# Row-maximum products in four row groups, a scalar form of the mask product, and a new order of the second pass in a four-layer graph network

## The reference

```python
h = jnp.maximum(_layernorm(x, axis=-1), 0.0)
Q = (h @ Wq.T).reshape(b, n, H, DH).transpose(0, 2, 1, 3)      # H = 8, DH = 32; K and V likewise
scores = jnp.einsum('bhnd,bhmd->bhnm', Q, K) / jnp.sqrt(jnp.float32(DH))
scores = jnp.where(adj[:, None, :, :] == 0, -jnp.inf, scores)
attn = jax.nn.softmax(scores, axis=-1)
out = jnp.einsum('bhnm,bhmd->bhnd', attn, V)
x = x + out.transpose(0, 2, 1, 3).reshape(b, n, H * DH) @ Wo.T + bo
```

## Time and profile before

| what | value |
|---|---|
| median of 3 runs | 3994.09 us (3990.95 to 3995.72) |
| span of the profiled execution | 3982.8 us |
| PE busy | 3709.5 us, 93% |
| DVE busy | 3101.9 us, 78% |
| ACT busy | 1994.8 us, 50% |
| POOL busy | 1576.2 us, 40% |
| share of PE in the chain that ended last | 78% |

### The profile page before, as it was taken

One profiled execution on the slowest core, in us unless ns is written; L12 is line 12 of the kernel. 1 busy time (PEld: TensorE's weight loads), 2 busy tenths in 40 slices (PEclk: granted clock), 3 DMA queues, 4 the chain that ended last, 5 costly groups with the idle time before them and its releaser, 6 DMA issues.

```text
span 3982.8 us, 59433 instructions
## 1 busy us (share of the span) xinstructions
PE 3709.5 (93%) x19042; PEld 2707.6 (68%) x19042; DVE 3101.9 (78%) x5637; ACT 1994.8 (50%) x3047; POOL 1576.2 (40%) x980
## 2 busy tenths in 40 slices
PE   7999579999999999999999999999999999999986
PEld 6888346676667766666666676766677666666665
DVE  6787557888887888888888888888878888888752
ACT  4656145555555555555545545555555555555430
POOL 4667234333443444444433333334434444444310
PEclk9999689999999999999999999999999999999986
DMA  8988322222222212222222222222222212222200
GB/s 286 317 310 298 93 53 64 70 69 69 63 58 69 60 52 56 53 69 69 69 69 69 69 69 69 69 69 63 58 69 59 58 52 53 69 69 69 53 16 11
DMA packets 195935, 341.10 MB, mean 86 GB/s; under 512 B 28720, under 2 KB 64432, under 8 KB 195888
## 3 DMA queue, kind: packets, MB, share of 16 engines
q1 hardware_dynamic: 195888, 340.50, 30.3%
HBM read 188.89 MB, written 50.33 MB: 60 GB/s over the span
## 4 chain that ended last, share of the span: by engine, by line
PE 78%; DVE 10%; ACT 4%; issue 3%; POOL 2%; DMA 2%; SPq 1%; DVEq 0%; ACTq 0%; POOLq 0%
PE bank L1444 12%; PE bank L1495 12%; PE obank L1378 12%; PE bank L1233 9%; PE pair L1233 7%; PE pair L1362 7%; PE bank L1406 6%; PE bank L1463 3%; PE pair L1339 3%; DVE minus_max L1033 2%; PE obank L1265 2%; DMA pT<-in_adjT 2%; PE bank L1265 1%; DVE b_st L841 1%; ACT hsq L632 1%
## 5 line engine op out<-in xcount | busy, mean ns | idle before, releaser
L602 POOL TENSOR_TENSOR pT<-pT,node_edge 128x1024 f32<-128x1024 f32 x256 | 628.6, 2462 | 532.0 <-ACT pT L690 530.1
L690 ACT ACTIVATE pT<-pair 128x1024 f32<-128x1024 f32 x512 | 515.9, 1031 | 325.6 <-PE obank L1378 248.2
L1033 DVE TENSOR_REDUCE minus_max<-pair 128x2 f32<-128x1024 f32 x512 | 603.3, 1216 | 56.9 <-PE pair L1339 56.5
L1023 DVE TENSOR_TENSOR pT<-pT,node_edge 128x1024 f32<-128x1024 f32 x256 | 399.8, 1562 | 269.4 <-ACT pT L690 266.2
L1495 PEld LDWEIGHTS bank<-v,p3T 128*128 128x128 f32 x4096 | 502.4, 199 | 36.2 <-DVE p3T L1182 24.5
L1495 PE MATMUL bank<-v,p3T 128*128 128x65 f32 x4096 | 499.8, 280 | 20.2 <-DVE p3T L1182 20.2
L540 POOL TENSOR_TENSOR d_rs<-d_ve,minus_half 128x4 f32<-128x4 f32 x32 | 32.2, 1007 | 1207.5 <-DVE d_ve L853 1207.5
L1378 PE MATMUL obank<-pT,v 128*64 128x512 f32 x2048 | 490.3, 611 | 8.4 <-POOL pT L602 4.8
L1444 PE MATMUL bank<-w_s,hid 128*128 128x256 f32 x2048 | 479.6, 389 | 0.3 <-DVE hid L1112 0.3
L1444 PEld LDWEIGHTS bank<-w_s,hid 128*128 128x128 f32 x2048 | 383.6, 192 | 87.7 <-issue 40.1
L632 ACT ACTIVATE p3T<-x,d_sh,d_rs 128x256 f32<-128x256 f32 x128 | 66.4, 589 | 720.6 <-POOL d_sh L546 720.6
(11 more groups left out here) (189 smaller groups left out, 6468.7 us busy)
## 6 DMA issues: line engine op xcount, KB each, us to landing
pT<-in_adjT SPq DMA_DIRECT2D x64, 512.0 KB, 5.3
a_at<-in_adjT SPq DMA_DIRECT2D x64, 512.0 KB, 3.6
q_parts<-high_parts SPq DMA_DIRECT2D x256, 128.0 KB, 4.7
k_parts<-high_parts SPq DMA_DIRECT2D x256, 128.0 KB, 4.1
b_at<-in_adjT SPq DMA_DIRECT2D x64, 512.0 KB, 3.9
hid<-in_x SPq DMA_DIRECT2D x32, 512.0 KB, 4.4
x_res<-hid SPq DMA_DIRECT2D x32, 512.0 KB, 5.0
pre_bn<-hsq SPq DMA_DIRECT2D x32, 512.0 KB, 4.1
```

What stands on the lines that cost most here:

```text
L602: nc.gpsimd.tensor_tensor(half, half, node_edge[:, 0:2, :], ALU.mult).then_inc(a_masked[0].sem, 1)
L690: nc.scalar.activation(dst, pair[p][:, :, :], func, **more).then_inc(a_copied[p].sem, 1)
L1023: nc.vector.tensor_tensor(half, half, node_edge[:, 2:4, :], ALU.mult).then_inc(a_masked[1].sem, 1)
L1033: nc.vector.tensor_reduce(minus_max[:, t, 2 * two_heads:2 * two_heads + 2], pair[p][:, :, :], AX.X, ALU.max, negate=True).then_inc(a_copie ...
```

## The change

There are three edits.

1. `a.nat{j}` now makes four products, from rows 0, 32, 64 and 96, and fills both `pair` tiles. There are 8 such steps instead of 16. A step first waits until both tiles are free. `a.max{j}{p}` reads tile p. The number of products and of reductions stays.
2. The DVE half of the mask product is a `scalar_tensor_tensor` with a factor of 1.0 instead of a `tensor_tensor`. The result is the same.
3. `ORDER` is a new list: other positions, and other lags, for about all steps.

```diff
@@ a_mask on DVE @@
-                    nc.vector.tensor_tensor(half, half, node_edge[:, 2:4, :], ALU.mult).then_inc(a_masked[1].sem, 1)
+                    nc.vector.scalar_tensor_tensor(out=half, in0=half, scalar=1.0, in1=node_edge[:, 2:4, :], op0=ALU.mult,
+                                                   op1=ALU.mult).then_inc(a_masked[1].sem, 1)
@@ a_nat on PE @@
-            def a_nat(h, q):
-                two_heads, t = divmod(2 * h + q, T)
+            def a_nat(j):
+                chunk, t = divmod(j, T)
 
                 def f(g):
 
                     pe.wait_ge(*a_high_ok.upto(g, 2))
-                    dst, full = a_free(g, U_NAT + 2 * h + q)
-                    for b in range(2):
-                        chunk, r = divmod((2 * two_heads + b) * DH1, P)
-                        i = nc.tensor.matmul(dst[:, b, :], q_high[r:r + DH1, chunk, t * P:(t + 1) * P],
-                                             k_high[r:r + DH1, chunk, :], start=True, stop=True)
-                    i.then_inc(full, 1)
+                    into = [a_free(g, U_NAT + 2 * j + p) for p in range(2)]
+                    for p, (dst, full) in enumerate(into):
+                        for b in range(2):
+                            r = (2 * p + b) * DH1
+                            i = nc.tensor.matmul(dst[:, b, :], q_high[r:r + DH1, chunk, t * P:(t + 1) * P],
+                                                 k_high[r:r + DH1, chunk, :], start=True, stop=True)
+                        i.then_inc(full, 1)
@@ ORDER, its first line before and after @@
-a.exp00:2 a.max11:1 a.max20:1 a.scores11:1 b.hid3:2 b.hidc1:3 a.exp01:2 a.max21:1 b.rrms:3 b.hidc2:3 a.scores20:1
+a.values00:1 b.x30:3 a.exp31:2 a.values01:1 a.max31:1 b.sumsq4:2 a.scores30:1 b.hidc5:3 a.max30:1 b.hid4:2 b.x31:3
```

More of the change, by code:

```diff
@@ L74 @@
[L74 to L78, removed]
@@ L89 @@
-h.head3:3
+a.values00:1 b.x30:3 a.exp31:2 a.values01:1 a.max31:1 b.sumsq4:2 a.scores30:1 b.hidc5:3 a.max30:1 b.hid4:2 b.x31:3
+b.hidc6:3 h.values00:3 a.load:0 b.stats3:3 p.rstd:0 h.values01:3 a.exp40:2 a.xmid0:2 a.scores31:1 b.hid5:2 a.max40:1
+a.headc1:2 h.spread1:3 a.edges1:1 b.sumsq5:2 b.hidc7:3 a.scores40:1 a.max41:1 b.hid6:2 a.exp41:2 a.xmid1:2
+a.values10:1 b.stats:2 a.values11:1 a.exp50:2 b.sumsq6:2 b.eye:2 b.hid7:2 p.sortq:1 a.exp51:2 a.scores41:1 a.max51:1
+a.scores50:1 a.max50:1 p.norm:1 a.mask4:1 h.values10:3 a.max60:1 h.values11:3 a.exp60:2 a.max61:1 a.scores51:1
@@ new lines @@
+b.factors:3 a.exp61:2 a.scores60:1 b.sumsq7:2 a.max71:1 b.sum:2 a.exp70:2 h.spread2:3 a.max70:1 a.scores61:1 b.low:3
+a.headc2:2 a.values20:1 a.mask5:1 p.sortk:1 b.vcol:3 p.flipc:1 a.values21:1 b.aggl0:2 b.spread:2 a.exp71:2 b.aggl1:2
+a.scores70:1 b.rrms:2 b.v3c0:3 h.values20:3 b.tanh0:3 p.flip:0 b.v3c1:3 a.scores71:1 b.tanh1:3 a.vmask0:1 h.values21:3
+a.mask6:1 h.prob0:3 p.qhigh:1 a.values30:1 a.vmask1:1 p.q0:0 b.tanh2:3 a.putshift:1 p.x1:0 h.spread3:3 a.mask7:1
+a.vmask2:1 p.q1:0 a.headc3:2 a.values31:1 h.head0:3 p.khigh:1 p.k0:0 a.vmask3:1 p.k1:0 h.prob1:3 b.tanh3:3 b.bias:2
@@ L90 @@
+a.nat7:0 b.sumsq1:1 a.exp10:1 b.silu1:2 b.agg1:1 p.klow:0 b.vt:2 b.hidc1:2 a.load1:0 a.shift:0 b.silu2:2 a.exp11:1
+a.mask2:0 b.v30:2 b.silu3:2 b.hid0:1 b.edges:2 b.hidc2:2 a.scores00:0 a.max01:0 a.scores01:0 a.exp20:1 b.sumsq2:1
+a.max00:0 b.v31:2 a.max11:0 b.hidc3:2 a.scores10:0 b.hid1:1 a.max10:0 a.exp30:1 h.spread0:2 a.mask3:0 a.edges0:0
+b.load:1 a.scores11:0 a.exp21:1 h.head3:3 b.hid2:1 a.max21:0 b.hidc4:2 b.hid3:1 b.sumsq3:1 a.max20:0 a.scores20:0
+a.headc0:1 a.div1:1 a.scores21:0
 """.split()
@@ L1205, in _ @@
                 "p.qlow": a_low(0, U_Q, q_high, q_low), "p.klow": a_low(1, U_K, k_high, k_low), **{f"a.xmid{q}": a_wo(q) for q in range(2)},
[L1206 removed]
+                **{f"a.max{j}{p}": a_max(j, p) for j in range(K * T) for p in range(2)},
                 **{f"a.vmask{h}": a_mask(h) for h in heads1}, **{f"a.div{k}": a_div(k) for k in range(K)},
@@ L1505, in _ @@
                 **{f"p.v{q}": a_v(q) for q in halves}, **{f"a.wo{q}": a_wo(q) for q in halves},
-                **{f"a.nat{h}{q}": a_nat(h, q) for h in heads1 for q in halves},
+                **{f"a.nat{j}": a_nat(j) for j in range(K * T)},
                 **{f"a.scores{h}{q}": a_scores(h, q) for h in heads1 for q in halves},
```

27 lines of the change are left out of this document (9 added, 18 removed).

## The result

The changed kernel takes 4307.73 us in the median of 4 runs (4302.28 to 4310.05), the kernel before 3993.76 us (3990.95 to 3995.72). The ratio is 1.0782, with a 95% interval of 1.0767 to 1.0798. The change makes the kernel slower, as forecast, but by 314 us and not by 181: the time lies 133 us above the prediction and 73 us above the upper end of its range.

What follows compares the result with a forecast made beforehand. SP's chain through a.load was taken to delay the first scores: 16.0 + 33.5 + 61.2 = 110.7 us a graph, with clock 111.9, or 6.05 more, 30 times 181 us; predicted 4175 us, range 4020 to 4235.

Steps and rivals of the forecast that it cites:

- The products: PE's first stretch, first product to last b.out2: four-product steps save 0.30 us each, 17.24 to 16.0 us.
- the four later steps: Four of a graph's eight product steps, lying where PE waits anyhow: no saving counted.
- The mask product: DVE's mask product, eight a graph: new form changes nothing, -0.1 to +0.15 us each; 11.0 us idle hides the worse end.
- rule of half throughput: Skill's rule for DVE's form with two non-bf16 SBUF sources: by it some 9.8 us a graph more DVE work.
- E + 33.5: First scores' start, E being the first b.agg's start: sort and shift held behind a.load; previously E + 29.2 or 27.6.
- the four points on the way: Chain after E: a.xmid1 ends at 7.6, a.bias at 10.05, sort's first issue at 11.3, sort issued by 26.9 us.
- Everything behind the scores: Stretch 4, first scores to next graph's first a.nat, taken as all PE: 59.8 + 1.45 = 61.2 us.
- The clock: PE's granted clock drops: 1.2 us a graph as before, possibly nothing or up to some 3.4.
- A: Rival: PE bounds, order harmless, products give 2.4 us a graph; 3922 us; chance 0.08.
- C: Rival: gains and idle time cancel, sort in time, shift's wait under 2.5 us; 3994 us; chance 0.04.
- B: Rival: sort in time but shift late, PE idles 3.5 us more and gains 2.4; 4027 us; chance 0.08.
- D: Rival: four products don't run side by side, first stretch stays 17.24, same SP chain; 4211 us; chance 0.05.

Runs made afterwards that it cites:

- e9: Changed kernel with its order, but products in steps of two in two row groups as before; 4332.99 us, ratio 1.085 to the kernel before.
- e3: Kernel before, own order, with four products at a time in place of the second of each two steps; 4002.79 us, ratio 1.0024.
- e5: Kernel before with only the scalar form of DVE's mask product; 3994.07 us, ratio 1.0005.
- e6: Changed kernel with the old form of DVE's mask product; 4303.02 us, ratio 1.0778 to the kernel before.
- e1: Changed kernel with SP's a.load of the next graph moved behind this graph's sort; 4223.94 us, ratio 1.058 to the kernel before.
- e2: Kernel before with both sort steps moved behind the next graph's a.load on SP; 4504.58 us, ratio 1.1284.
- e7: e4 with POOL's mask product cut to 64 of its 1024 columns a partition; 4170.45 us, ratio 1.0446 to the kernel before.
- e4: Changed kernel with 28 constant products keeping PE busy ahead of the wait for the first scores; 4261.84 us, ratio 1.0666 to the kernel before.
- e13: Kernel before with POOL's mask product cut to 64 of 1024 columns a partition; 3992.49 us, ratio 0.9996.
- e8: e4 with full work and DVE's a.vmask6 moved behind b.scale1; 4237.62 us, ratio 1.0616 to the kernel before.
- e15: Changed kernel, a.load behind the sort, b.hid1 and b.v31 ahead of first scores, POOL's mask product cut; 4079.07 us, ratio 1.0221.

## Why the prediction was right and where it failed

- **The products.** I took 0.30 us a step and 16.0 for the stretch. Measured are 0.22 and 16.49. It was mis-sized: the four cost what the pair in the earlier trace rows costs (0.44 and 0.43), and another 0.13 us lie ahead of the fifth step. That the four later steps give nothing was right for the time (e9), but in e3 they cost 0.42 us.
- **The mask product.** "The form changes nothing" holds (e5, e6). The rule of half throughput that I had weighed against it is for two sources that are not bf16. The mask product has one bf16 source and can't test it; the product of two f32 sources in the earlier trace rows speaks against it, with 1225 ns. "The same median" did not come: it is 1331 ns in the changed kernel against 1226, and 1331 in e6 too, so it goes with the order. What I added was wrong: that DVE's idle time in the last stretch hides long cases. Under the new order it does not.
- **The order, up to the scores.** E + 33.5 was forecast, and E + 32.95 came in the graph shown (33.11 in the mean), with the four points on the way within 0.4 us (7.6 and 7.2, 10.05 and 9.7, 11.3 and 10.9, 26.9 and 26.8). PE's wait was 6.62 us, inside 5 to 8. e1 and e2 confirm the cause.
- **Everything behind the scores: the step that failed.** "PE is in order, so everything behind the scores moves with them: 61.2 us to the next `a.nat`." It took 65.9. PE's work there is as reckoned (e7 has 60.9 with all of it), but I treated it as pure PE, while its order on DVE and POOL was also new. Late results of DVE cost 2.9 us (e4 to e7). Under the old order the same cut gives nothing (e13). That the mutual hold-up of DVE and POOL makes DVE late is shown for one product (e8, 1.3 us of stretch 4); for all of them it rests on e7, with the open side told there.
- **The clock.** I took 1.2 us and named 3.4 as the worst. The half clock behind the standstill costs 2.1 us in stretch 4 (e4). So it was mis-sized by 0.9, within its bounds.
- **The sum.** +0.5 for the products, -0.4 for the scores, +4.7 for stretch 4, less the 1.2 that I had set apart: 3.6 us a graph, 108 of the 133 us. The other 25 are terms of the count: 12 for the intervals (300.5 - 181 - 108), 21 ahead of the loop's first `a.shift` and behind its last, which I had put at nothing without a reason, and 8 less, because the median lay 3.2 us above the profiled span and not 11.3.
- **Rivals.** A and C fell with e1 and e2. B's wait exists (e1), but not as the first one. D is out: the four do run side by side.

Left open: why stretch 4 gains more than PE's listed waits for DVE lose (2.9 for 1.9 in e7; e15 gained 3.6).
